# Second attention of a macaron network: the row maxima reach the queries by a small transfer, and the extra work is placed anew

## What is computed

```
qkv = (layernorm(x) @ w_qkv).reshape(B, L, 3, H=16, D=8).transpose(2, 0, 3, 1, 4)
q, k, v = rope(qkv[0]), rope(qkv[1]), qkv[2]
attn = softmax(einsum('bhqd,bhkd->bhqk', q, k) * D**-0.5, axis=-1)
out = einsum('bhqk,bhkd->bhqd', attn, v)
x = x + out.transpose(0, 2, 1, 3).reshape(B, L, C) @ w_proj + b_proj
```

## Time and profile before

| | |
|---|---|
| median of 3 runs | 2680.11 us (2675.53 to 2683.67) |
| the profiled execution, its own time | 2689.33 us |
| its span | 2687.6 us |
| TensorE matmul busy, share of the span | 2304.1 us, 86% |
| VectorE | 2038.6 us, 76% |
| ScalarE | 1321.5 us, 49% |
| GpSimd | 927.6 us, 35% |
| mean granted TensorE clock | 0.921 |

### The profile page before, as it was taken

One profiled execution on the slowest core, in us unless ns is written; L12 is line 12 of the kernel. 1 busy time (PEld: TensorE's weight loads), 2 busy tenths in 40 slices (PEclk: granted clock), 3 DMA queues, 4 the chain that ended last, 5 costly groups with the idle time before them and its releaser, 6 DMA issues.

```text
span 2687.6 us, 39104 instructions
## 1 busy us (share of the span) xinstructions
PE 2304.1 (86%) x11234; PEld 1569.8 (58%) x11234; DVE 2038.6 (76%) x4733; ACT 1321.5 (49%) x1911; POOL 927.6 (35%) x836
## 2 busy tenths in 40 slices
PE   4499467769589999949999999999999996999999
PEld 3377356547477777725545454545554553787777
DVE  6588577658489999847777777777777774888887
ACT  0188222258444444425555555555555554444444
POOL 6600666410267777621111111111111100556554
PEclk9999555579789999959999999999999998999999
DMA  6343111044188888911111111111111111788897
GB/s 163 102 134 113 35 34 32 20 134 153 53 184 173 178 183 172 191 46 51 56 52 53 52 51 51 51 51 51 51 51 51 54 52 32 165 185 177 177 188 156
DMA packets 142703, 265.92 MB, mean 99 GB/s; under 512 B 21004, under 2 KB 24079, under 8 KB 142335
## 3 DMA queue, kind: packets, MB, share of 16 engines
q1 hardware_dynamic: 134174, 247.44, 38.5%
q0 software_dynamic: 8416, 17.25, 2.5%
HBM read 212.44 MB, written 54.27 MB: 99 GB/s over the span
## 4 chain that ended last, share of the span: by engine, by line
PE 59%; DVE 14%; issue 10%; ACT 7%; DMA 6%; SPq 2%; POOL 1%; POOLq 1%; DVEq 0%; ACTq 0%
PE ps L1863 12%; PE ps L1887 9%; PE ps L1607 7%; PE ps L1609 7%; PE ps L1608 7%; PE ps L1874 6%; DMA gate_rows<-gates_dram 4%; DVE shift L1485 3%; DVE m L1322 2%; ACT g L809 2%; PE ps L1621 1%; ACT g_hi L782 1%; PE ps L1936 1%; PE ps L1614 1%; PE ps L1634 1%
## 5 line engine op out<-in xcount | busy, mean ns | idle before, releaser
L1485 DVE TENSOR_REDUCE shift<-ps 128x1 fp32r<-128x512 f32 x1024 | 670.8, 686 | 122.8 <-PE ps L1863 120.8
L927 ACT ACTIVATE prob<-ps 128x1024 f32<-128x1024 f32 x512 | 522.4, 1025 | 411.3 <-PE ps L1874 403.9
L782 ACT ACTIVATE hi<-m 128x512 fp32r<-128x512 f32 x512 | 318.9, 631 | 414.9 <-DVE m L1322 414.8
L1863 PE MATMUL ps<-k_pad,q_st 128*128 128x512 f32 x1024 | 418.8, 451 | 81.5 <-DVE shift L1485 65.9
L628 POOL TENSOR_TENSOR lo<-m,hi 128x512 fp32r<-128x512 f32 x256 | 341.4, 1335 | 308.2 <-ACT hi L782 307.5
L1322 DVE SCALAR_TENSOR_TENSOR m<-ps,gate_rows 128x512 f32<-128x512 f32 x512 | 335.3, 681 | 91.5 <-PE ps L1609 47.0
L1863 PEld LDWEIGHTS ps<-k_pad,q_st 128*128 128x128 f32 x1024 | 181.6, 191 | 370.5 <-DVE shift L1485 329.2
L1874 PE MATMUL ps<-q_sh,k_pad 128*128 128x512 f32 x1024 | 329.1, 403 | 0.0
L1887 PE MATMUL ps<-prob,v_cols 128*32 128x512 f32 x2048 | 275.8, 611 | 0.4 <-ACT prob L927 0.4
L604 POOL TENSOR_SCALAR var_eps<-meanvar 128x4 f32<-128x4 f32 x48 | 11.1, 230 | 675.0 <-DVE meanvar L1041 674.0
L1006 DVE TENSOR_TENSOR lo<-m,hi 128x512 fp32r<-128x512 f32 x256 | 208.5, 815 | 16.4
(11 more groups left out here) (213 smaller groups left out, 3949.4 us busy)
## 6 DMA issues: line engine op xcount, KB each, us to landing
gate_rows<-gates_dram SPq DMA_DIRECT2D x256, 512.0 KB, 6.5
w_blk<-w_dram SPq DMA_DIRECT2D x38, 514.5 KB, 3.7
q_st<-q_dram SPq DMA_DIRECT2D x64, 256.0 KB, 2.6
k_dram<-qk_hl SPq DMA_DIRECT2D x48, 256.0 KB, 3.0
q_dram<-qk_hl SPq DMA_DIRECT2D x48, 256.0 KB
k_pad<-k_dram SPq DMA_DIRECT2D x256, 48.0 KB
x_blk<-sorted_x SPq DMA_DIRECT2D x38, 256.0 KB, 3.5
sorted_y<-yb_rows SPq DMA_DIRECT2D x38, 256.0 KB, 2.0
```

Of the source, the lines that this page charges most:

```text
L782: return act.activation(o, i, ACT.Copy)
L927: act.activation(prob[:, h % HP, 2 * half:2 * half + 2, :], ps[:, b0:b0 + 2, :], ACT.Exp, scale=SCALE).then_inc(sig(ph, "prob"), 1)
L1485: dve.tensor_reduce(shift[:, g % 2, b, c:c + 1], wide(PASS1 + b % 2), AXX, ALU.max, negate=True).then_inc(sig(ph, "qmax"), 1)
L1863: pe.matmul(wide(PASS1 + b % 2), q_st[:, g % 2, b * P:b * P + P], k_pad[:, HPG * g + j], start=True, stop=True).then_inc(sig(ph, "s1"), 1)
```

## The change

- `AHEAD` goes from 5 to 6 and `EARLY` from 9 to 10.
- `shift` becomes 16 columns a group; `shifted` is one matmul with a 16x128 result. `shifted_queries` and `q_sh` are gone. ScalarE copies the 16x128 result out (`shift_out`) and issues a DMA that writes it into rows 24 of the four heads in `q_st`, which gets a buffer for each group. `pass2` reads `q_st` and waits for that DMA; the load of `q_st` waits for no reader of its own.
- On VectorE every extra piece now stands between the first two and the last two maxima of its step, or behind them.
- The visits to the shared bank are in new places.
- GpSimd makes the normalised rows (`apply_norm4`, two instructions), two tiles ahead; the moments are taken at steps 10 to 12; `bias` moves behind the rope pieces.
- Two semaphores each are merged into one (`unstaged`, `consts`); the startup of the attention waits accordingly.

```diff
-AHEAD = 5
-EARLY = 9
+AHEAD = 6
+EARLY = 10
-        q_st = late_sb("q_st", [P, 2, SEQ], F32R)
-        q_sh = late_sb("q_sh", [P, 2, SEQ], F32R)
-        shift = late_sb("shift", [P, 2, BLK, P], F32R)
+        q_st = late_sb("q_st", [P, GROUPS, SEQ], F32R)
+        shift = late_sb("shift", [P, 2, HPG, BLK], F32R)
+        shift_rows = late_sb("shift_rows", [HPG * BLK, P], F32R)
...
@@ SyncE, load_group @@
-                if again or g > 1:
-                    pass_wait(sp, sig(4, "qsh_sb"), t * GROUPS + g - 1)
...
@@ GpSimd @@
+                    def apply_norm4(t, first=False):
+                        pass_wait(pool, sig(4, "rstd"), t + 1)
+                        if not first:
+                            pass_wait(pool, sig(4, "tr"), t)
...
+                        pool.tensor_tensor(xn[:], xt, meanvar[:, :, 0:1].broadcast_to(every),
+                                           ALU.subtract).then_inc(sig(4, "centred"), 1)
+                        pool.wait_ge(sig(4, "centred"), t + 1)
+                        pool.tensor_tensor(xn[:], xn[:], rstd[:].unsqueeze(2).broadcast_to(every),
+                                           ALU.mult).then_inc(sig(4, "xn"), 1)
...
                     def body4(t, p, more):
-                        if more:
-                            rstd_of(4)(t + 1, 1 - p)
-                            ahead4(t + 1, 1 - p)
+                        if two_more(t):
+                            rstd_of(4)(t + 2, p)
+                            apply_norm4(t + 2)
+                            ahead4(t + 2, p)
...
@@ ScalarE @@
+                def shift_out(t, g):
+                    n = t * GROUPS + g
+                    act.wait_ge(sig(ph, "qsh"), n + 1)
+                    if not (isinstance(t, int) and t == g == 0):
+                        act.wait_ge(sig(ph, "q_shift"), n * 16)
+                    copy(shift_rows[:], ps[0:HPG * BLK, MISC, 0:P]).then_inc(sig(ph, "srow"), 1)
+                    pass_wait(act, sig(ph, "srow"), n + 1)
+                    act.dma_start(q_st[3 * HD:P:32, g, :].bitcast(F32), shift_rows[:].bitcast(F32))\
+                       .then_inc(sig(ph, "q_shift"), 16)
...
+                    if h in (4, 6) and more:
+                        rope_high(n, q, (h - 4) // 2)
                     exps(t, h, 0)
-                    if h == 6 and more:
-                        rope_high(n, q, 0)
-                    if h == 12 and more:
+                    if h == 0 and more:
+                        head_a(n, q)
+                    if h == 13 and more:
                         head_b(n, q)
+                    if h == 8 and before is not None:
+                        project(before)
                     exps(t, h, 1)
-                    if h == 2 and before is not None:
-                        project(before)
-                    if h == 3 and more:
-                        head_a(n, q)
-                    if h == 7 and more:
-                        rope_high(n, q, 1)
+                    if h in (2, 6, 10):
+                        shift_out(t, (h + 2) // HPG)
+                    if h == 14 and more:
+                        shift_out(n, 0)
...
@@ VectorE, step (shifted_queries removed) @@
                     ahead = h + AHEAD
                     if ahead < HEADS or more:
                         maxima(t + ahead // HEADS, ahead % HEADS // HPG, ahead % HPG, (0, 1))
+                    if h in (1, 3, 4, 5) and more:
+                        rotary(n, (1, 3, 4, 5).index(h))
+                    if h == 7 and before is not None:
+                        output(before, GROUPS - 1)
+                    if h == 9 and before is not None:
                         add_projected(before)
+                    if h in (11, 12, 15):
+                        output(t, (11, 12, 15).index(h))
                     if ahead < HEADS or more:
                         maxima(t + ahead // HEADS, ahead % HEADS // HPG, ahead % HPG, (2, 3))
+                    if two_on and h in (10, 11):
+                        moments_of(t + 2, (2 * (h - 10), 2 * (h - 10) + 1))
+                    if two_on and h == 12:
+                        moments_done(t + 2)
...
@@ TensorE @@
-                        pe.wait_ge(sig(ph, "qsh_sb"), t * GROUPS + g + 1)
+                        pe.wait_ge(sig(ph, "q_shift"), (t * GROUPS + g + 1) * 16)
...
-                def shifted(t, g, p):
+                def shifted(t, g):
                     pe.wait_ge(sig(ph, "qmax"), (t * GROUPS + g + 1) * 16)
-                    for b in range(BLK):
-                        last = pe.matmul(rows4(MISC)[:, b], shift[:, g % 2, b], ident_r[:], start=True, stop=True)
-                    last.then_inc(sig(ph, "qsh"), 1)
+                    pe.matmul(ps[0:HPG * BLK, MISC, 0:P], shift[:, g % 2].rearrange("p j b -> p (j b)"), ident_r[:],
+                              start=True, stop=True).then_inc(sig(ph, "qsh"), 1)
```

More of the change, by code:

```diff
@@ L1526, in add_projected, with moments_of, moments_done, step @@
                        .then_inc(sig(ph, "x_done"), 4)
-                def step(t, p, h, more, before=None):
-                    n = t + 1
-                    if h == 2 and before is not None:
-                        output(before, GROUPS - 1)
-                    if h in (9, 14):
-                        output(t, {9: 0, 14: 2}[h])
-                    if h in (5, 7) and more:
-                        rotary(n, {5: 0, 7: 3}[h])
+                def moments_of(t, blocks):
+                    if blocks[0] == 0:
+                        dve.wait_ge(sig(ph, "xn"), t)
+                        pass_wait(dve, sig(3, "x_done"), t * 4 + 4)
+                    for b in blocks:
+                        last = dve.bn_stats(stats[:, b, :], x_block(ph, t, b))
+                    if blocks[-1] == BLK - 1:
+                        last.then_inc(sig(ph, "stats"), 1)
+                def moments_done(t):
+                    pass_wait(dve, sig(ph, "stats"), t + 1)
+                    for b in range(BLK):
+                        last = dve.bn_aggr(meanvar[:, b, :], stats[:, b, :])
+                    last.then_inc(sig(ph, "meanvar"), 1)
+                def step(t, p, h, more, before=None, two_on=False):
+                    n = t + 1
                     ahead = h + AHEAD
@@ L1862, in pass1 @@
                             pe.wait_ge(sig(ph, "qmax"), (t * GROUPS + g) * 16 + 4 * j + b - 1)
[L1863 removed]
+                        pe.matmul(wide(PASS1 + b % 2), q_st[:, g, b * P:b * P + P], k_pad[:, HPG * g + j],
                                   start=True, stop=True).then_inc(sig(ph, "s1"), 1)
@@ L1874, in pass2 @@
                         last = pe.matmul(wide(PASS2 + j), k_pad[:, HPG * g + j, kb * P:kb * P + P],
-                                         q_sh[:, g % 2], start=True, stop=True)
+                                         q_st[:, g], start=True, stop=True)
                     last.then_inc(sig(ph, "st"), 1)
@@ L1954, in early_work, with late_work @@
                         else:
-                            bank_read("qsh_sb", g4 + 2)
-                        shifted(t, 2, p)
+                            bank_read("srow", g4 + 2)
+                        shifted(t, 2)
+                    if h == 10:
+                        shifted(t, 3)
+                    if h == 14 and more:
+                        bank_read("v_cols", n + 1)
+                        shifted(n, 0)
+                def late_work(t, p, h, more, before):
+                    n, q, g4 = t + 1, 1 - p, t * GROUPS
+                    if h == 2 and more:
+                        bank_read("srow", g4 + 2)
+                        head_qk(n, q, 1)
+                    if h in (3, 4) and more:
+                        bank_read("qk_read", n * 4 + h - 1)
+                        head_qk(n, q, h - 1)
+                    if h == 6 and before is not None:
+                        bank_read("srow", g4 + 3)
+                        o_rows(before, GROUPS - 1)
+                    if h == 7 and before is not None:
+                        attended(before)
@@ L1957, in early_work @@
                     if h == 8 and before is not None:
-                        bank_read("qsh_sb", g4 + 3)
                         project(before)
                     if h == 10:
+                        bank_read("srow", g4 + 4)
+                        o_rows(t, 0)
+                    if h == 11:
                         bank_read("o_all", g4 + 1)
                         o_rows(t, 1)
-                    if h == 11:
+                    if h == 12 and more:
                         bank_read("o_all", g4 + 2)
-                        shifted(t, 3, p)
@@ L2008, in late_work @@
+                    if h == 14:
+                        if more:
+                            bank_read("srow", g4 + 5)
+                        else:
+                            bank_read("o_all", g4 + 2)
                         o_rows(t, 2)
@@ L2021, in step @@
                         pass1(t1, g, j, (3,))
```

(2 more changed lines are left out.)

169 lines of the change are left out of this document (57 added, 112 removed).

## The result

The changed kernel takes **2577.05 us** (median of 4 runs, 2573.05 to 2579.33) against 2679.98 for the kernel before, measured beside it: ratio 0.9615, 95% interval 0.9595 to 0.9635, so 103 us less. The forecast was 2590, 90 less. The profiled execution took 2573.05, 4.0 under its median, where the one before stood 9.2 above its own.

The account below looks back on a forecast made before the run. Each attention step was taken as held by a loop of TensorE and VectorE. Terms 92.2 - 1.4 + 0.9 + 3 - 2.6 - 2 = 90 us, off 2680.11, gave 2590 us; range 2572 to 2638.

Parts of the forecast that it names:

- The rule: Attention stretch: takes the larger of 3.41 and 3.04 plus visits ahead of b2, plus what stands in the middle.
- The tile: One attention tile of sixteen stretches: falls from 64.55 to 58.4 us, 6.15 less.
- The shift matmul in the middle: Stretches 2, 6, 10, 14: one uncovered matmul, taken as 0.12 each, bounded by nil and 0.40.
- VectorE's fullness: Stretches 11 and 12: VectorE holds 3.7 against 3.49; nil to 0.4 in all, taken as 0.15.
- The stall of the first qk visit: TensorE waits for GpSimd's low part: nil to 0.62, taken as 0.35.
- The fifteen periods: Fifteen attention tile periods at 6.15 each: 92.2 us gained, less 1.4 at tile 0, plus 0.9 at tile 15.
- signs named: Changed kernel's trace: tile 58 to 59, no stretch above 4.3, stretch 1's qk visit waits 0.3, TensorE waits name no DMA.
- The loop's turn: Stretch 10 at six turns: maxima start at 3.83, costing 2.30 against 1.86 before; 2.6 lost in all.
- The ends: Attention's startup and last tile: about 3 gained in the last tile, 2 lost at startup.
- The new wait: `pass2` waits for copy plus DMA: landing taken as 2.6, slack 0.9 to 1.9 a group, no cost.
- The rival of a late transfer: The shift's DMA lands late, the slower side: 2750 us at a landing of 6.5; chance 0.03.
- The order of completions: Group 2's transfer may wait for query-piece stores until 5.5, perhaps half a microsecond a tile: sum 82, not 90; left open.

Follow-up runs that it names:

- outputs_first: The changed kernel with the four `output` calls put back ahead of the first two maxima: 2639.95 us, ratio 0.9843.
- order_only: The kernel before with one edit, VectorE's extra pieces moved behind the first two maxima, still five heads ahead: 2622.72 us, ratio 0.9777.
- ahead_five: The changed kernel with `AHEAD` at 5 in place of 6: 2644.77 us, ratio 0.9866.
- halves_together: The changed kernel with the second `pass2` half put ahead of b2 in every step: 2565.24 us, ratio 0.9568.
- issue_after_exp: The changed kernel with ScalarE's DMA issue one step later, also waiting on the semaphore of that step's second exponential: 2690.73 us, ratio 1.0037.
- shift_on_vector: The changed kernel with the shift's old route, four matmuls and VectorE's addition to the queries, no copy or DMA on ScalarE: 2597.18 us, ratio 0.9687.
- issue_later: The changed kernel with ScalarE's DMA issue one step later, behind the second exponential in program order only: 2581.19 us, ratio 0.9627.
- v_at_turn: The changed kernel with the v visit moved from step 12 to the end of step 9, its copy ahead of step 10's first exponential: 2568.02 us, ratio 0.9582.

## Why the prediction was right, step by step

- **The size.** The forecast fell 13 us short of the 103 saved. The terms below missed nearly all to the same side, so no error hid another.
- **The rule** for a stretch (the larger of 3.41 and 3.04 plus the visits ahead of b2) holds. It gave 3.49, 3.73, 3.98 and 3.94, and the trace has 3.48 to 3.50, 3.73 to 3.75, 3.94 and 3.93. outputs_first and order_only show its condition, VectorE's pieces behind the first maxima; ahead_five shows a second that the prediction did not state, that the shift matmul must not need the maximum of its own step. halves_together shows that the 3.41 belongs to this order of the matmuls (3.31 there).
- **The tile** was put at 58.4 and took 57.90. The shift matmul in the middle costs 0.05 and not 0.12 (3.46 against 3.41): 0.28 a tile. VectorE's fullness, taken as 0.15, costs nothing; stretch 12 has 3.32 busy in 3.48. The stall of the first qk visit is 0.31 where 0.35 was taken. The fifteen periods without the turns gave 98.9, where 92.2 - 1.4 + 0.9 = 91.7 stood: 7.2 of the miss. Of the signs named, the plain tile is thus just below the 58 to 59; the other sizes of stretches came as named, the stall of stretch 1 too, and the only waits on a DMA are outside the groups' transfers.
- **The loop's turn** is the term with the wrong sign. I had 2.6 lost, and 4.1 were gained: the excess of the six turns fell from 17.45 to 13.3. Two steps failed. VectorE starts over in 2.34 to 2.67, and not in the 2.89 of the earlier trace rows, so that the maxima start 3.14 to 3.47 into the stretch and not at 3.83; and I priced the turn of before by stretch 9 alone, while in four of its six turns the stretch behind took 4.8 to 5.1 in place of 3.48 at a lower granted clock. After the change that happens in two. The range held this miss of 6.7 easily.
- **The ends.** The startup lost 0.7 (2 taken), the last tile gained 3.24 (3 taken), and what follows its last `values` lost 0.9 (6.46 to 7.37). That last is not the change's doing: the last project's eight matmuls took 2.07 at a granted clock of 0.50 in this execution and 1.16 at 1.00 before, and they take 1.16 in ten of the experiments' twelve profiles.
- **The new wait.** Copy 0.25 (0.3 taken), issue 0.54 (0.35 taken), and wanted at 5.98, 5.41, 5.41 and 5.05 into the stretch (6.1, 5.6, 5.6, 5.1 taken). The landing, which the trace of before could not give, was taken as 2.6; issue_after_exp has it at 1.8 in a quiet moment and at up to 3.2 beside the 256 KB load. Against 3.96 to 4.88 from issue to use at least 0.8 is spare, so the cost of nil was right. The rival of a late transfer has the mechanism right, and issue_after_exp is it: with the issue some 3.7 us later (1.33 into stretch 0 in place of 1.09 into stretch 15), nothing is left of the gain.
- **The order of completions.** I had left open whether group 2's transfer would wait for the stores of the query pieces, as the rule of the Trainium skill (DMA: Bandwidth & Descriptors, section Queues, rings and completion order) has it. No run settles the rule: in the changed kernel these stores were complete when the load that waits for them went, at 1645.03 in the tile above, 0.9 ahead of `pass2`, and ahead of it in every other tile that has such a load (by 0.1 to 1.2), so that the transfer is in time by either. What issue_after_exp shows, for group 0, is simpler: the packets of the transfer themselves move later, behind those of another queue.
- **The whole.** Against 90 stand 104.7 in the attention: 7.2 from the tile, 6.7 from the turns, 1.3 from the startup, 0.2 from the last tile, less 0.9 behind its last `values`. Taking the 9.2 between the profiled execution and the median over was right: 2680 less 103 is the measured median, and 116 less is only what the two profiled executions show.

Of the 103 us, the order on VectorE is worth 57 (order_only). The new placement with six ahead, and all else that changed with it (GpSimd's share is at most 5), bring 25 more (shift_on_vector against order_only), and the shift's new route 20. Taken away one at a time, the order of the outputs costs 63 and six ahead 68, each in four stretches of its own (7, 11, 12 and 15; 2, 6, 10 and 14). These prices don't add up to the gain, since each is that of one part missing in the new placement: with five ahead the shift waits in the middle of its step, a wait which the kernel before didn't have there. No run took both away.

## What to carry to other kernels

When two engines hand one bank to and fro, find the instruction that the loop waits for, and put behind it on both engines whatever can stand behind it; here a step with such a piece then cost TensorE's own time and nothing else. Price a loop's turn over the stretches that follow it as well. A small transfer on a queue of its own is cheap when it has 4 us to land, but leave room for a large one that passes ahead of it.

## What the runs showed of the hardware that was not expected

- A DMA issue on ScalarE's queue went out 0.12 to 0.15 ahead of an exponential that stands before it in the program, 60 times in 64 (issue_later). With a wait on that instruction's semaphore it came after it (issue_after_exp).
- An issue took 0.54 on ScalarE and 0.35 on SyncE, in the same kernel.
- 8 KB from one buffer of the core to another landed in 1.8 when alone (from the start of the issue to the matmul that waits), and up to 3.2 beside a 256 KB load issued 0.17 later, whose packets went first.
- At the loop's turn VectorE was idle for 2.34 to 2.67 in the changed kernel, 2.88 to 2.93 before, and 1.96 to 2.18 in halves_together, where its last maximum before the turn ends 0.36 later and the first one behind it starts 3.1 to 3.3 into the stretch (3.1 to 3.5 in the changed kernel). So this is no fixed price behind the last piece. In each of the six turns of the kernel before, the changed one and five others looked at, one or two packets of an instruction queue (q14) move within that idle time. That VectorE waits there for its instructions fits, but the profile doesn't say whose they are, and why 2.3 and 2.9 differ is open.
- At the loop's turn the granted clock fell from 2.4 to 1.2 GHz in four of six cases after TensorE had sat idle for 2.65 to 2.70 (before), in two of six after 1.68 to 2.02 (the changed kernel), in none after 0.78 to 1.04 (v_at_turn). Over all fourteen kernels it fell in 20 of the 60 turns with 1.6 or more idle and in none of the 24 with 1.21 or less. Among the 60 the idle time alone doesn't decide it: in the changed kernel it fell after 1.72 and 1.68, and not after 2.02.
